# A transformer block on one Trainium2 core: a bound moved to GpSimd, gathers ahead of a flag, late loads a block later, and first quads woven in

## The reference, cut to what matters

```
w = exp(-(pos[..., None] - centers) ** 2 / (2.0 * exp(log_variances)))
w_top, idx = top_k(w, 10);  h = sum over the ten of w_top/sum(w_top) * embeddings[idx]
h = h + attention(layernorm(h))    # 8 heads over 2 kv heads, low-rank q and kv, rope, causal
h = h + ffn(layernorm(h))          # router, 42 of 64 experts, gelu, hidden 256
```

## Time and profile before

| what | us |
|---|---|
| median of 3 runs | 1882.8 (1880.69 to 1885.8) |
| the profiled execution's own time | 1883.86 |
| its span, first to last instruction | 1881.8 |
| PE busy | 1775.4 (94%) |
| DVE busy | 1566.0 (83%) |
| ACT busy | 1515.1 (81%) |
| POOL busy | 1419.3 (75%) |

### The profile page before, as it was taken

One profiled execution on the slowest core, in us unless ns is written; L12 is line 12 of the kernel. 1 busy time (PEld: TensorE's weight loads), 2 busy tenths in 40 slices (PEclk: granted clock), 3 DMA queues, 4 the chain that ended last, 5 costly groups with the idle time before them and its releaser, 6 DMA issues.

```text
span 1881.8 us, 29932 instructions
## 1 busy us (share of the span) xinstructions
PE 1775.4 (94%) x8424; PEld 1424.6 (76%) x8424; DVE 1566.0 (83%) x2190; ACT 1515.1 (81%) x2685; POOL 1419.3 (75%) x855
## 2 busy tenths in 40 slices
PE   5478699997999999999999999999999999999998
PEld 4355467765788888888888888888888888888886
DVE  8549788888688888888888888888888888888888
ACT  2268688884888888888888888888888888888886
POOL 4423076676499889888888888688888888888886
PEclk9889799996999999999999999999999999999999
DMA  7410000003533333333333333333333333333332
GB/s 232 144 55 18 1 1 0 0 4 76 137 113 113 134 120 115 120 135 113 115 136 115 111 133 118 112 115 136 112 114 136 112 112 135 115 111 135 116 112 67
DMA packets 99864, 192.91 MB, mean 103 GB/s; under 512 B 13766, under 2 KB 76214, under 8 KB 83638
## 3 DMA queue, kind: packets, MB, share of 16 engines
q1 hardware_dynamic: 97742, 187.82, 29.6%
q0 software_dynamic: 2048, 4.20, 0.7%
HBM read 179.40 MB, written 12.58 MB: 102 GB/s over the span
## 4 chain that ended last, share of the span: by engine, by line
PE 78%; DVE 6%; ACT 2%; issue 2%; POOL 2%; POOLq 0%; DVEq 0%; ACTq 0%
PE f_ps_h L2421 12%; PE f_ps_h L2422 12%; PE f_ps_h L2423 12%; PE f_ps_y L2434 12%; PE f_ps_y L2435 12%; PE f_ps_y L2436 12%; PE ps_s L1639 2%; DVE neg_max L1510 2%; PE ps_p L1592 1%; PE ps_ko L1625 1%; POOL y_sum L2273 1%; PE ps_qy L1582 1%; PE ps_qy L1600 1%; DVE g_lo L2375 1%; DVE q_t L1479 1%
## 5 line engine op out<-in xcount | busy, mean ns | idle before, releaser
L2273 POOL TENSOR_TENSOR y_sum<-y_sum,weighed 128x512 f32<-128x512 f32 x504 | 1027.9, 2050 | 102.6 <-DVE weighed L2367 95.4
L2375 DVE TENSOR_TENSOR g_lo<-gelu_out,g_hi 128x1024 fp32r<-128x1024 f32 x512 | 817.3, 1596 | 84.9 <-ACT g_hi L2314 68.3
L2305 ACT ACTIVATE gelu_out<-f_ps_h,b_t 128x512 f32<-128x512 f32 x1024 | 648.5, 685 | 194.8 <-PE f_ps_h L2423 194.0
L2314 ACT ACTIVATE g_hi<-gelu_out 128x1024 fp32r<-128x1024 f32 x512 | 541.9, 1059 | 0.0
L2367 DVE SCALAR_TENSOR_TENSOR weighed<-f_ps_y,b_t,c_row 128x512 f32<-128x512 f32 x504 | 375.5, 745 | 120.5 <-PE f_ps_y L2436 119.5
L2421 PE MATMUL f_ps_h<-x_hi,w_hi 128*128 128x512 f32 x1024 | 399.6, 390 | 4.7 <-ACT e L1863 4.7
L2434 PE MATMUL f_ps_y<-g_hi,w_hi 128*128 128x512 f32 x1024 | 400.1, 391 | 3.0 <-DVE g_lo L2375 2.4
L2422 PE MATMUL f_ps_h<-x_lo,w_hi 128*128 128x512 f32 x1024 | 399.4, 390 | 0.0
L2423 PE MATMUL f_ps_h<-x_hi,w_lo 128*128 128x512 f32 x1024 | 399.2, 390 | 0.0
L2435 PE MATMUL f_ps_y<-g_lo,w_hi 128*128 128x512 f32 x1024 | 398.5, 389 | 0.0
L2436 PE MATMUL f_ps_y<-g_hi,w_lo 128*128 128x512 f32 x1024 | 398.4, 389 | 0.0
(11 more groups left out here) (244 smaller groups left out, 1543.5 us busy)
## 6 DMA issues: line engine op xcount, KB each, us to landing
c_row<-comb_rows SPq DMA_DIRECT2D x124, 1024.0 KB, 4.9
w_raw<-in_w SPq DMA_DIRECT2D x256, 128.0 KB, 4.4
c_row<-comb_rows SPq DMA_DIRECT2D x16, 256.0 KB, 5.6
by_slot<-b_zeros SPq DMA_DIRECT2D x1, 3072.0 KB, 13.7
out<-h SPq DMA_DIRECT2D x8, 256.0 KB, 4.2
cent<-in_centers SPq DMA_DIRECT2D x1, 1536.0 KB
neg_prec<-in_logvar SPq DMA_DIRECT2D x1, 1536.0 KB
b_gauss_s<-by_slot SPq DMA_DIRECT2D x6, 256.0 KB, 4.4
```

The source lines that it names most:

```text
L2273: pool.tensor_tensor(y_sum[:, w, g, :], y_sum[:, w, g, :], weighed[:, r % 2, :], ALU.add).then_inc(added, 1)
L2305: last = act.activation(gelu_out[:, r % GELUS, c, :], ps_h[:, r % 2, c, :], ACT.Gelu, bias=b_t[:, c, bass.ds(e, 1)])
L2314: act.activation(g_hi[:, r % RING], gelu_out[:, r % GELUS], ACT.Copy).then_inc(hi_ready, 1)
L2375: dve.tensor_tensor(g_lo[:, r % RING], gelu_out[:, r % GELUS], g_hi[:, r % RING].bitcast(F32), ALU.subtract).then_inc(lo_ready, 1)
```

## The change

Six parts, with line numbers of the kernel before.

1. `far`, the bound of the other blocks, is computed on GpSimd, in nine instructions of 128x768 ahead of the first scatter. The edges now go through ps_turned and an ACT copy to SBUF (`edges_all`). DVE keeps the reduction to `nearest`, moved from behind the last quad to the head of quad 1, where it waits for `far_ready`.
2. ACT does copy_turned(0), copy_turned(1) and copy_mixed(0) ahead of exponentials(7).
3. SP issues the six loads of the late slots in `front`, behind the barrier, and no longer ahead of it.
4. POOL gathers all 16 early tiles at the start of "tower", ahead of the test of the flag. (In the general program the early rows are written straight into `h`; DVE waits there for the gathers.) In `front` it waits for the late stores and gathers tiles 16 to 31; tiles 12 to 15 no longer wait for `kv_mean_ready`.
5. PE does turn_late(0) ahead of the product of W_VR and W_O.
6. Quad 0's norm, copy, latents, sums and squares, and quad 1's norm, are woven into late steps 1 to 4, and the loop over quads starts at s=1.

```diff
@@ embed_by_block, SP: taken out
-            sp.wait_ge(scattered[1], 16 * HALF_TILES)
-            load_slots(sp, by_slot, 1, late_s, late_in)
@@ embed_by_block, POOL: ahead of the scatters
+            mark, settle, link = chain(pool, far_step, 0)
+            low, high, weakest = (edges_all[:, k * BLOCKS:(k + 1) * BLOCKS].unsqueeze(2)
+                                  .broadcast_to([P, BLOCKS, TILES]) for k in range(3))
+            position = tokpos[:, 1, :].unsqueeze(1).broadcast_to([P, BLOCKS, TILES])
+            pool.wait_ge(edges_copied, 1)
+            pool.wait_ge(counted, 1)
+            mark(pool.tensor_tensor(far[:], low, position, ALU.subtract))
+            mark(pool.tensor_tensor(beyond[:], position, high, ALU.subtract))
+            settle()
+            mark(pool.tensor_scalar(far[:], far[:], 0.0, None, ALU.max))
+            link(pool.tensor_scalar(beyond[:], beyond[:], 0.0, None, ALU.max))
+            link(pool.tensor_tensor(far[:], far[:], beyond[:], ALU.add))
+            link(pool.tensor_tensor(far[:], far[:], far[:], ALU.mult))
+            mark(pool.tensor_tensor(far[:], far[:], weakest, ALU.mult))
+            link(pool.tensor_scalar(beyond[:], own[:], MASKED, None, ALU.mult))
+            pool.tensor_tensor(far[:], far[:], beyond[:], ALU.add).then_inc(far_ready, 1)
@@ embed_by_block, ACT
             squares(0)
-            for q in range(QUADS):
-                if q + 1 < QUADS:
-                    squares(q + 1)
-                else:
-                    copy_turned(0)
-                exponentials(q)
-            for i in range(LOADS_OF_HALF):
+            act.wait_ge(edges_spread, 1)
+            act.activation(edges_all[:], ps_turned[:, 0:3 * BLOCKS], ACT.Copy).then_inc(edges_copied, 1)
+            for q in range(QUADS - 1):
+                squares(q + 1)
+                exponentials(q)
+            copy_turned(0)
+            copy_turned(1)
+            copy_mixed(0)
+            exponentials(QUADS - 1)
+            for i in range(1, LOADS_OF_HALF):
@@ embed_by_block, DVE: at the head of the loop over quads; L612 to L618 are taken out
+                if q == 1:
+                    dve.wait_ge(far_ready, 1)
+                    mark(dve.tensor_reduce(nearest[:], far[:].rearrange("p b t -> p t b"), AX.X, ALU.max))
@@ embed_general, POOL
             pool.sem_clear(spent)
+            for k in range(HRING):
+                pool.wait_ge(stored[k], 16 * STORES_OF_HALF)
+            for t in range(HALF_TILES):
+                gather_rows(pool, h, t, source, mixed_rows, rows_back)
             engine_program(pool, "pool", body)
@@ front, SP: ahead of the late stores
+            sp.wait_ge(scattered[1], 16 * HALF_TILES)
+            load_slots(sp, by_slot, 1, late_s, late_in)
@@ front, POOL
-            for t in range(TILES):
-                if t % HALF_TILES == 0:
-                    for k in range(HRING):
-                        pool.wait_ge(stored[k], 16 * STORES_OF_HALF * (t // HALF_TILES + 1))
-                if t % QUAD == 0 and t // QUAD >= AHEAD:
+            for k in range(HRING):
+                pool.wait_ge(stored[k], 16 * STORES_OF_HALF * HALVES)
+            for t in range(HALF_TILES, TILES):
+                if t % QUAD == 0:
                     pool.wait_ge(kv_mean_ready, t // QUAD - AHEAD + 1)
+                gather_rows(pool, h, t, source, mixed_rows, rows_back)
@@ front, ACT
             for i in range(LOADS_OF_HALF):
-                if i == LATE_BEHIND:
+                if i + 1 < LOADS_OF_HALF:
+                    copy_late_turned(i + 1)
+                copy_late_mixed(i)
+                if i == 1:
                     root_x(0)
                     norm_x(0)
-                if i + 1 < LOADS_OF_HALF:
-                    copy_late_turned(i + 1)
-                if i == LOADS_OF_HALF - 1:
+                if i == 2:
                     copy_x(0)
-                copy_late_mixed(i)
-            root_x(1)
-            norm_x(1)
-            for s in range(QUADS + 1):
+                if i == 3:
+                    copy_c(0)
+                if i == 4:
+                    root_x(1)
+                    norm_x(1)
+            copy_x(1)
+            root_kv(0)
+            root_x(2)
+            norm_x(2)
+            for s in range(1, QUADS + 1):
@@ front, PE
+            turn_late(0)
             pe.wait_ge(vr_copied, 1)
...
-            turn_late(0)
             for i in range(LOADS_OF_HALF):
                 if i + 1 < LOADS_OF_HALF:
                     turn_late(i + 1)
-                else:
+                mix_late(i)
+                if i == 2:
                     turn_x(0)
-                mix_late(i)
-            for s in range(QUADS + 1):
+                if i == 3:
+                    latents(0)
+                if i == 4:
+                    sums(0)
+            turn_x(1)
+            for s in range(1, QUADS + 1):
```

More of the change, by code:

```diff
@@ L207, in make_router @@
                                    router_rev, router_b_rev, mv, rstd, x_hi, x_lo, comb_t, y_sum, f, b_t)
-                last_heads = front(nc, block, mid, h, ident, ones, w, w_loaded, wsum, rsum, source, late_s, late_in,
-                                   e["table"], mixed, mixed_rows, stored, rows_back, qk, v_all, rms, rms_ready, res_added, tile_copied)
+                last_heads = front(nc, block, mid, h, ident, ones, w, w_loaded, wsum, rsum, source, by_slot, scattered,
+                                   late_s, late_in, e["table"], mixed, mixed_rows, stored, rows_back, qk, v_all, rms, rms_ready, res_added, tile_copied)
                 router, qk_normed, y_ready, mv_copied = attend(
@@ L608, in _ @@
                                              ).then_inc(chosen, 1)
-            dve.wait_ge(edges_spread, 1)
-            low, high, weakest = (over_tiles(ps_b[:, edges_at][:, k * BLOCKS:(k + 1) * BLOCKS]) for k in range(3))
-            position = over_blocks(tokpos[:, 1, :])
-            dve.tensor_tensor(far[:], low, position, ALU.subtract)
-            link(dve.tensor_tensor(beyond[:], position, high, ALU.subtract))
-            link(dve.tensor_tensor(far[:], far[:], beyond[:], ALU.max))
-            link(dve.scalar_tensor_tensor(out=far[:], in0=far[:], scalar=0.0, in1=far[:], op0=ALU.max, op1=ALU.mult))
-            link(dve.tensor_tensor(far[:], far[:], weakest, ALU.mult))
-            link(dve.scalar_tensor_tensor(out=far[:], in0=own[:], scalar=MASKED, in1=far[:], op0=ALU.mult, op1=ALU.add))
-            link(dve.tensor_reduce(nearest[:], far[:].rearrange("p b t -> p t b"), AX.X, ALU.max))
             link(dve.tensor_tensor(nearest[:], nearest[:], top_b[:, :, TOPK - 8], ALU.max))
@@ L653, in _ @@
             pe.wait_ge(edges_ready, 1)
-            pe.matmul(ps_b[:, edges_at], ones[0:BLOCKS, :], edge_diag[:].rearrange("b a c -> b (a c)"), start=True,
+            pe.matmul(ps_turned[:, 0:3 * BLOCKS], ones[0:BLOCKS, :], edge_diag[:].rearrange("b a c -> b (a c)"), start=True,
                       stop=True).then_inc(edges_spread, 1)
@@ L762, in body @@
                 act.wait_ge(tile_done, TILES)
[L763 to L765 removed]
+                act.dma_start(mixed_rows[1][HALF_SLOTS:, :].rearrange("(t p) d -> p t d", p=P),
+                              h[:, HALF_TILES:, :]).then_inc(rows_out, 16)
             engine_program(act, "act", body)
@@ L775, in body @@
             def body(pool):
-                for k, first in ((0, 0), (1, HALF_SLOTS)):
-                    pool.iota(source[:, k * HALF_TILES:(k + 1) * HALF_TILES], pattern=[[P, HALF_TILES]], base=first,
-                              channel_multiplier=1)
+                pool.iota(source[:, HALF_TILES:], pattern=[[P, HALF_TILES]], base=HALF_SLOTS, channel_multiplier=1)
                 pool.wait_ge(prec, 1)
@@ L814, in body @@
             def body(dve):
+                for q in range(HALF_TILES // QUAD):
+                    dve.wait_ge(rows_back[q], 16 * QUAD)
                 dve.memset(wsum_out[:], 1.0)
@@ L855, in _, with front @@
             engine_program(pe, "pe", body)
-def front(nc, block, signals, h, ident, ones, w, w_loaded, wsum, rsum, source, late_s, late_in, table, mixed,
-          mixed_rows, stored, rows_back, qk, v_all, rms, rms_ready, res_added, tile_copied):
+def front(nc, block, signals, h, ident, ones, w, w_loaded, wsum, rsum, source, by_slot, scattered, late_s, late_in,
+          table, mixed, mixed_rows, stored, rows_back, qk, v_all, rms, rms_ready, res_added, tile_copied):
     QUADS = TILES // QUAD
```

29 lines of the change are left out of this document (15 added, 14 removed).

## The result

| | before | after |
|---|---|---|
| median of 8 runs each, us | 1882.65 (1880.69 to 1885.8) | 1888.67 (1883.92 to 1891.22) |
| the profiled execution: its own time, its span | 1883.86, 1881.8 | 1891.22, 1889.4 |

A forecast was written before the change was run, and what follows sets the result against it. PE holds 78% of the chain, but only the first 124 us could move. 5.1 - 2.6 - 2.8 - 1.6 - 0.8 - 2.0 = -4.7 gave 1879.2 profiled, median 1878.1 us; range 1869 to 1886.

The forecast's parts named there:

- The term of part 4: Early gathers at the start of the tower: value 0, between +1 and -0.5 us, with GpSimd's later branch hidden.
- the gain of the other parts, -9.8: All terms but the bound on GpSimd, from early mix to weave, together save 9.8 us.
- Part 1, +5.1: Embedding, quad 1 on DVE: waits 3.6 us for GpSimd's chain, then reduces for 1.5; bounds +1.5 and +18.7 us.
- few two-tensor instructions: Embedding, 14 to 28 us: DVE has few such instructions, so GpSimd's chain was taken at 14.1 us.
- Rival A: GpSimd's chain and DVE's wait at quad 1: both engines block each other, up to +8.9 us, 1891.7; chance 0.18.
- rival C: Early and late mix: two unexplained ACT gaps vanish under another order, total -10.9 us, 1871.9; chance 0.20.
- 4.86 us for a quad: Embedding up to 68 us: DVE sets the pace, starting quads 1 and 2 4.86 us apart.
- Part 2, -2.6: Early mix at quad 7: copies ahead of the exponentials save nearly one step, 2.6 us, between 0 and 3.0.
- Part 3, -2.8 at the barrier and -1.6 at the restart: Barrier 2.8 us earlier without six load issues; PE's restart 1.6 us shorter, as code gets ahead of late slots' data.
- rival B: Restart and weave bring little: code still waits for data, woven steps stall; -1.1 us, 1881.7; chance 0.22.
- Part 5, -0.8: Late mix start: turn_late(0) fills PE's idle time while DVE copies turned W_VR, saving 0.8 us, between 0 and 1.1.
- Part 6, -2.0: Last late copy to first copy_tile: 5.8 us leaves, late steps 2 to 5 take 3.8 longer; net -2.0 us.

The follow-up runs named there:

- a1: The kernel before with part 1 alone added (bound on GpSimd, its reduction at quad 1); 1889.65 us, ratio 1.0035 to before.
- u1: The changed kernel with part 1 alone undone (bound back on DVE behind the last quad); 1882.77 us, ratio 0.9992 to before.
- a4: The kernel before with part 4 alone added (all 16 early tiles gathered ahead of the flag); 1890.08 us, ratio 1.0034 to before.
- the hold: The changed kernel without parts 1 and 4, early gathers cut into runs of four by two waits; 1868.98 us, and 1864.47 us in another group.
- h3: The hold with part 3 undone (late slots' loads issued ahead of the barrier again); 1874.06 us, ratio 0.9957 to before.
- u6: The changed kernel with part 6 alone undone (no weave in the late steps); 1890.19 us, ratio 1.0036 to before.
- h6: The hold with part 6 undone (no weave in the late steps); 1873.96 us, ratio 0.9957 to before.
- c14: The changed kernel with parts 1 and 4 undone (bound on DVE, 12 early tiles gathered in the front); 1874.02 us, ratio 0.9949 to before.
- lr: The hold with GpSimd fetching the sixteen late tiles in one run after a single wait; 1887.85 us, ratio 1.0022 to before.

## Why the prediction was wrong

Two steps failed. The term of part 4 was put at nothing, and it came to 5 to 7 us, because a longer run of gathers makes PE's signals late. And the gain of the other parts, -9.8, was set against a price for part 1 whose path was wrong, though its size was nearly right.

**Part 1, +5.1.** The step that failed is what stood for DVE: a wait of 3.6 us for GpSimd and 1.5 for the reduction. The reduction was right (1.43). GpSimd's chain came out longer, its six two-tensor instructions at 1.47 to 1.85 us, the three with one tensor at about 2.15 and not 1.17, and it ended at 30.8 and not at 28.3. Nobody waited for it, as DVE came at 31.7: its own placement chain had been shut out for 6.9 us, for which my working had "few two-tensor instructions". I counted them by their length. A short one pays up to a whole instruction of GpSimd, 1.4 us for 0.2, and one-tensor ones, which I didn't count at all, make up half of the 6.9. Rival A named the mechanism, but at the wrong place (GpSimd's instructions hardly grew, DVE stood still) and at too high a price, and had 0.18. Of the 8.3 at quad 1, 5.8 are left at quad 7; the price in the end is 5.9 (a1, u1). That 5.1 and 5.9 lie close is luck: a wait of 3.6 that didn't come was in the sum, and 6.9 that did come were not.

**Part 4, 0.** This is the largest error: -5.0 when undone, +7.0 alone. I had asked what the gathers contend with (the DMA engines, GpSimd's own branch), and when their rows are wanted, but not what GpSimd's run of indirect DMAs does to others' signals. Yet the rows had it: rival C spoke of two gaps that nothing explained, and said nothing shows what they hang on. Both lie while GpSimd is in such a run, the one among scatters, the other among gathers; from 120 us on, with gathers in fours, there were none. The look that was missing was GpSimd's line beside each unexplained gap. C expected that another order may lose them; part 4 made the run longer by a third, and the gaps grew from 6.9 to 11.0 us alone (a4) and to 13.4 in after.

The reading of the embedding had the same gap in it. I wrote that DVE sets the pace with 4.86 us for a quad, but eight such quads from 19.89 on end at 58.8, and DVE left the last one at 67.97. Late signals beside scatters (quads 2 and 5, above) make up most of that difference.

**Part 2, -2.6.** Not to be seen in after: from quad 7 to the last copy_mixed 19.05 us before, 20.3 after. The early mix had 8.8 us of late signals where before had 6.9, beside scatters that are issued until 78.6. Even in the hold its worth isn't settled.

**Part 3, -2.8 at the barrier and -1.6 at the restart.** The first is right: 3.1 by h3. The second failed. From the barrier to PE's first product are 4.8 us in after, 5.1 before, and 4.7 and 5.1 in the hold and h3: 0.3 gained on the branch, not 2.3. The code does not wait behind the slots' data, or not only; rival B had this at 0.22.

**Part 5, -0.8.** Not measured by itself. In the traces the first product of the late mix starts 4.6 us behind PE's restart in after, 5.5 before, which fits.

**Part 6, -2.0.** 1.5 in after (u6), within the error. In the hold between 1.8 and 5.7, by whether the late signal in h6 is counted.

**The sum.** Parts 2, 3, 5 and 6 together were -9.8 and came to -9.0 by the medians (c14), with the restart short and part 2 not to be seen; which of the others made up for them isn't shown. The two edits on GpSimd were +5.1 and 0, and came to some 6 and 5 to 7. So -9.0 + 5.9 + 7.0 = +3.9 by their lone effects, +6.0 as measured; the remainder is within the errors of four medians. Of the range, the low end was widened for gaps that may vanish, and the high end only for half of rival A; that gaps could grow ("new ones can come") was written and had no price. Two inputs of the working stand on no row: the 0.83 us for a one-tensor instruction in part 1's lower bound (2.12 to 2.19 measured), and rival C's 6.2 us, where the two gaps it names come to 9.3.

What stays open: in which part of the chip a long run of indirect DMAs holds back other engines' signals. Runs of four show nearly none of it (one late signal of 2.3 us, on DVE) and runs of eight some. How long the pause between two runs must be wasn't tried. Nor was a hold of the scatters, which stand behind the early mix's 6.9 us (before) and 8.8 us (after, hold) of late signals.

The best version measured is the hold: parts 2, 3, 5 and 6 without 1 and 4, gathers in fours. At 1868.98 and 1864.47 us in two groups it is 0.8 to 1.0% faster than before and 20 to 24 us faster than after.

## What to carry to other kernels

Before work goes to an idle GpSimd, count the instructions of DVE beside it, the tiny ones and those with one tensor too: each can wait for a whole one of GpSimd's. Before transfers with computed addresses are issued early, look at how long a run without a break they form, and hold them with a wait that is there anyway, so that each quad's rows come when they are wanted. And a gap that no work explains belongs beside the lines of all other engines before a change that touches one of them is priced at nothing.

## What the runs showed of the hardware

- Signals come late while GpSimd issues indirect DMAs back to back. PE's to ACT in the late mix: the longest gap 3.9 to 7.9 us in runs of twelve or sixteen at 1.25 us each, 2.8 to 3.9 in runs of eight, none with runs of four; 14.3 us on ACT and 14.5 on DVE in a run of twenty. DVE's to itself: 3.3 and 2.7 us in a run of twelve scatters.
- The last late signal beside the late mix ends 1.0 to 3.1 us behind the run's last gather (1.6 before, 3.0 after, 3.1 in lr, 1.0 in h6).
- After such idle time PE's granted clock is 0.50 to 0.51 (c14, 100 to 108 us) where without it it is 1.00 (hold, 92 to 104).
- On GpSimd, with DVE at work beside it, an instruction with one tensor and constants took longer (128x768, 2.12 to 2.19 us) than one with two tensors (1.47 to 1.85).
- A DVE instruction of 128x32 with two tensors can last until an instruction of GpSimd that reads is over: 1.44 for 0.19 us. Fills of 0.74 us do not hold it up. One of 128x768 (L583) was not held up: 0.96 us as before. One-tensor instructions are held up by both (a cast of 128x32: 1.34 beside GpSimd's two-tensor ones, 0.70 beside fills, 0.18 alone).
- Behind the barrier the branch past a long program costs PE some 5 us, whether 1.5 MB of transfers lie ahead of it (5.1 in h3) or start beside it (4.7 in the hold).
